# A two-layer cross-attention and mixture-of-experts kernel: work moved between engines in the first routing, unread products, row stores and key transfers placed anew

## The reference, cut to what matters

```python
x = x + xattn(layernorm(x), ctx, ctx, ...)      # layer 0 attention, 16 heads of 8, 32 x 64 rows of 128
x = x + ffn0(layernorm(x), w_gate, w_g, w_u, w_d)  # routing: top 2 of 8 experts, softmax of the two
x = x + xattn(layernorm(x), ctx, ctx, ...)      # layer 1 attention
x = x + ffn1(layernorm(x), gate_w, W1, b1, W2, b2) # routing again, hidden 512, exact gelu, biases

def ffn1(x):
    topk_vals, topk_idx = top_k(xf @ gate_w, 2);  topk_w = softmax(topk_vals)
    comb = zeros.at[rows, topk_idx].add(topk_w)
    h = gelu(einsum('nd,edf->enf', xf, W1) + b1[:, None, :])
    return einsum('ne,end->nd', comb, einsum('enf,efd->end', h, W2) + b2[:, None, :])
```

## Time and profile before

| | us |
|---|---|
| median of 3 runs | 430.56 |
| runs | 435.54, 429.47, 430.56 |
| the profiled execution | 428.84 |
| its span, first to last instruction | 427.0 |
| PE busy in the span | 365.1 (85%) |
| DVE busy | 341.2 (80%) |
| ACT busy | 268.8 (63%) |
| POOL busy | 245.7 (58%) |

### The profile page before, as it was taken

The page is one execution under the profiler, slowest core; times in us unless marked ns, Lnnn a source line. Parts: engine busy times, 40 slices in busy tenths (PEclk is TensorE's granted clock), DMA queues, the critical chain, the costliest instruction groups (busy, mean ns, idle before and its releaser), DMA issues.

```text
span 427.0 us, 12926 instructions
## 1 busy us (share of the span) xinstructions
PE 365.1 (85%) x4528; PEld 256.8 (60%) x4528; DVE 341.2 (80%) x978; ACT 268.8 (63%) x591; POOL 245.7 (58%) x362
## 2 busy tenths in 40 slices
PE   3977799998779999999998799898878899999900
PEld 2644566666446656666655567676634798888800
DVE  6876589998888787887876689988877899999707
ACT  3664588987457555666556788786722766767504
POOL 7860367777525558576661244456787356677630
PEclk9996899999999999999999999998996999999965
DMA  7358797000001111101002400001113223232136
GB/s 202 83 166 257 218 382 266 4 3 2 2 0 51 51 52 49 48 16 40 0 11 34 62 3 2 5 21 34 40 47 102 78 79 95 78 90 65 45 103 223
DMA packets 30837, 33.15 MB, mean 78 GB/s; under 512 B 3908, under 2 KB 22606, under 8 KB 30776
## 3 DMA queue, kind: packets, MB, share of 16 engines
q1 hardware_dynamic: 27164, 25.84, 21.2%
q0 software_dynamic: 2496, 5.18, 3.6%
q10 hardware_dynamic: 1116, 1.31, 1.0%
HBM read 15.22 MB, written 15.01 MB: 71 GB/s over the span
## 4 chain that ended last, share of the span: by engine, by line
PE 48%; DVE 17%; SPq 10%; issue 10%; POOL 9%; ACT 3%; DMA 2%; POOLq 0%; DVEq 0%; ACTq 0%
PE ps L1433 10%; PE ps L1435 9%; PE ps L1434 9%; SPq L353 5%; PE ps L1681 4%; PE ps L1529 3%; DVE area L1026 3%; POOL sorted_rows L783 3%; POOL area L819 2%; PE ps L1602 2%; PE ps L1815 1%; SPq L371 1%; POOL expert_sums L839 1%; PE ps L1835 1%; PE ps L1443 1%
## 5 line engine op out<-in xcount | busy, mean ns | idle before, releaser
L819 POOL TENSOR_TENSOR area<-area 128x512 f16<-128x512 f32 x44 | 51.0, 1159 | 41.8 <-ACT area L587 41.8
L839 POOL DMA_INDIRECT expert_sums<-area x46 | 49.7, 1081 | 27.1 <-ACT area L609 14.4
L1433 PE MATMUL ps<-w,area 128*128 128x128 f16 (+1 forms) x360 | 63.7, 219 | 0.3 <-POOL area L819 0.2
L1434 PE MATMUL ps<-w,area 128*128 128x128 f16 (+1 forms) x360 | 63.7, 219 | 0.0
L1435 PE MATMUL ps<-w,area 128*128 128x128 f16 (+1 forms) x360 | 63.7, 219 | 0.0
L1433 PE MATMUL ps<-area,w 128*128 128x512 f16 (+1 forms) x180 | 58.8, 327 | 3.1 <-DVE area L1349 1.4
L1434 PE MATMUL ps<-area,w 128*128 128x512 f16 (+1 forms) x180 | 58.5, 325 | 0.0
L1435 PE MATMUL ps<-area,w 128*128 128x512 f16 (+1 forms) x180 | 58.4, 325 | 0.0
L1026 DVE TENSOR_REDUCE area<-ps 128x8 f32<-128x512 f32 x64 | 41.2, 686 | 14.5 <-PE ps L1681 13.2
L583 ACT ACTIVATE area<-ps 128x512 f32<-128x512 f32 x44 | 26.1, 597 | 35.1 <-PE ps L1435 34.5
L633 ACT ACTIVATE area<-ps,b_now 128x256 f32<-128x256 f32 x92 | 36.2, 477 | 12.0 <-PE ps L1435 11.9
(11 more groups left out here) (241 smaller groups left out, 1039.4 us busy)
## 6 DMA issues: line engine op xcount, KB each, us to landing
sorted_rows<-filler_rows SPq DMA_DIRECT2D x16, 528.0 KB, 6.3
w_stage<-in_L_ffn_W SPq DMA_DIRECT2D x8, 512.0 KB, 4.0
w<-sorted_rows SPq DMA_DIRECT2D x23, 132.0 KB
keys<-area SPq DMA_DIRECT2D x32, 48.0 KB
area<-in_ctx SPq DMA_DIRECT2D x4, 256.0 KB, 4.8
keys<-expert_sums SPq DMA_DIRECT2D x4, 256.0 KB, 5.4
keys<-expert_sums ACTq DMA_DIRECT2D x4, 256.0 KB, 6.2
out<-x_res SPq DMA_DIRECT2D x8, 128.0 KB, 1.9
```

What stands on the lines that cost most here:

```text
L819: nc.gpsimd.tensor_tensor(hid[:, n % 4, 1, :], gated[:, n % 4, :], hid[:, n % 4, 0, :], ALU.subtract).then_inc(q["lo"], 1)
L839: nc.gpsimd.indirect_dma_start(out=expert_sums, out_offset=bass.IndirectOffsetOnAxis(ap=to_row[:, j, h:h + 1], axis=0), in_=ys[j % OUTS][: ...
L1433: pe.matmul(dst, lhs[0], rhs[0], start=start, stop=False, **kw)
L1434: pe.matmul(dst, lhs[0], rhs[1], start=False, stop=False, **kw)
```

## The change

It has seven parts.

1. SP: `place_keys(0, 1)` is issued before the five tables and the first two weight chunks of layer 1, not behind them.
2. PE: 21 unread products are added between the projections and step 0 of attention 0 (2+2 in `project_queries`, 4 at the start, 6+2 in step -2, 2 in step -1, 3 in step 0). Fewer in the end of attention 1 (9 to 4, but 5 to 8 later) and at the start of `experts1` (7 to 3, 4 to 3).
3. ACT and POOL: `output_bias_rows` goes from the routing into steps 8 to 14 of the dense feed-forward, in three pieces (ACT) and four (POOL).
4. The lower halves of parts 0, 1 and 2 are made by PE (`take_part`: minus the upper half added to the bank) and ACT (`routing_low`), and no longer by DVE.
5. DVE: `rank` of part 0 stays in step 15, of part 1 goes behind the statistics of step 16, of part 2 behind the statistics of tile 15.
6. POOL: each entry of `STORED` comes one step earlier, and step 16 ends at 21 scatters, not 20.
7. DVE: `statistics(15)` before `row_shift(14)`; the late table in two, its second part behind `arrive(0)` and `arrive(1)`; `shares` behind the loop of `experts1`.

```diff
-STORED = {8: 2, 9: 4, 10: 6, 11: 9, 12: 11, 13: 14, 14: 16, 15: 18, 16: 20}
+STORED = {7: 2, 8: 4, 9: 6, 10: 8, 11: 11, 12: 13, 13: 16, 14: 18, 15: 20, 16: 21}
...
+            place_keys(0, 1)
             for dst, name in ((iota8, "iota8"), (expert_rows, "expert_rows"), (table, "table"), (before16, "before16"), (filler_rows, "filler")):
...
             load_chunk(1)
 
-            place_keys(0, 1)
...
+                    if l == 0 and t == TILES - 1:
+                        routing_low(F[l], 2)
...
                         routing_high(F[l], 2)
+                        routing_low(F[l], 0)
+                        routing_low(F[l], 1)
...
+            def routing_low(q, p):
+
+                t0, t1 = PARTS[p]
+                act.wait_ge(q["xt_sub"], p + 1)
+                nc.scalar.activation(xTa[:, 1, t0 * P:t1 * P], ps[:, part_bank[p], 0:(t1 - t0) * P], ACT.Copy).then_inc(q["xt_lo"], 1)
...
             def routing(l):
                 q = F[l]
-                output_bias_rows()
...
+                    if 8 <= n <= 10:
+                        output_bias_rows(n - 8)
...
-            def output_bias_rows():
-
-                pool.wait_ge(s["rs"], 2 * TILES)
+            def output_bias_rows(k):
+
+                e = slice(2 * k, 2 * k + 2)
                 pool.wait_ge(s["b2"], 34)
-                nc.gpsimd.tensor_tensor(b2_rows[32:33, :, :], b2_raw[32:33, :, :], b2_hi[32:33, :, :], ALU.subtract).then_inc(s["b2"], 1)
-                pool.wait_ge(s["b2"], 35)
+                pool.wait_ge(F[0]["lo"], 12 + k)
+                nc.gpsimd.tensor_tensor(b2_rows[32:33, e, :], b2_raw[32:33, e, :], b2_hi[32:33, e, :], ALU.subtract).then_inc(s["b2"], 1)
+                pool.wait_ge(s["b2"], 35 + k)
...
+                if 11 <= n <= 14:
+                    output_bias_rows(n - 11)
...
                     row_shift(LAST)
                     early_tiles()
-                    statistics(LAST + 1)
...
-                late_table()
-                shares()
+                tiles_left()
                 arrive(0)
                 arrive(1)
+                late_table()
...
+                if l == 0 and g >= 2:
+                    unread_products(2, 0, 0, 512)
                 pe.wait_ge(KV["xt"], n + 1)
...
+                        pe.wait_ge(KV["v_lo"], 2 * GROUPS)
+                        unread_products(6, 5, 0, 512)
+                    if l == 0 and t == 0:
+                        unread_products(3, 6, 0, 512)
...
                         turn_part(l, 2)
+                        take_part(l, 0)
+                        take_part(l, 1)
...
+            def take_part(l, p):
+
+                q = F[l]
+                t0, t1 = PARTS[p]
+                pe.wait_ge(q["xt_hi"], p + 1)
+                pe.matmul(ps[:, part_bank[p], 0:(t1 - t0) * P], minus_ident16, xTa[:, 0, t0 * P:t1 * P], start=False, stop=True,
+                          skip_group_check=True).then_inc(q["xt_sub"], 1)
...
-                unread_products(7, 5, 0, 512)
+                unread_products(3, 5, 0, 512)
                 turn(0)
                 turn(1)
-                unread_products(4, 6, 0, 512)
+                unread_products(3, 6, 0, 512)
```

More of the change, by code:

```diff
@@ L260, in build @@
         F = [sems("xh xt_ps xt_hi lg_ps lg top idx ex pr up act hi lo down "
-                  + ("gu xd xt_lo oh cb c16 ct_ps ct_a ct_d res t1 gt", "sa a16 rk_ps rk bs place tbl b1_ps b1 slots_ps xs_hi xs_lo gate y "
+                  + ("gu xd xt_sub xt_lo oh cb c16 ct_ps ct_a ct_d res t1 gt", "sa a16 rk_ps rk bs place tbl b1_ps b1 slots_ps xs_hi xs_lo gate y "
                      "tok nm wq sc ld0 ld1 ld2 ld3 so0 so1 so2 so3 so4 so5 so6 so7 sum0 sum1 sum2 sum3 add")[l], f"_f{l}") for l in range(2)]
@@ L557, in sort_rows @@
                 nc.scalar.activation(act_warm[:, 1:2], minus_half[:, :], ACT.Gelu)
[L559 to L565 removed]
+            def output_bias_rows(k):
+                if k == 0:
+                    act.wait_ge(s["b2"], 32)
+                    nc.scalar.activation(b2_rows[0:1, :, :], b2_raw[0:1, :, :], ACT.Copy, scale=WSCALE)
+                elif k == 1:
+                    nc.scalar.activation(b2_hi[32:33, :, :], b2_raw[32:33, :, :], ACT.Copy, scale=WSCALE).then_inc(s["b2"], 1)
+                else:
+                    act.wait_ge(s["b2"], 33)
+                    nc.scalar.activation(b2_raw[32:33, :, :], b2_raw[32:33, :, :], ACT.Copy, scale=WSCALE).then_inc(s["b2"], 1)
             def routing(l):
                 q = F[l]
[L569 removed]
                 routing_high(q, 3)
@@ L1004, in step @@
                         outputs(t - 1)
-                    if l == 0 and t == TILES - 1:
-                        low(F[l], 2)
-                    if l == 0 and t == TILES:
-                        rank(F[l], 1)
                     if alive(t + 1):
@@ L1012, in step @@
                         statistics(t - 2)
-                    if l == 0 and t == TILES - 2:
-                        low(F[l], 0)
-                    if l == 0 and t == TILES - 2:
-                        low(F[l], 1)
                     if l == 0 and t == TILES - 1:
@@ L1019, in step @@
                     if l == 0 and t == TILES:
-                        rank(F[l], 2)
+                        rank(F[l], 1)
                     if alive(t + 3):
@@ L1052, in last_steps @@
                     residual(LAST + 1)
+                    statistics(LAST + 1)
                     row_shift(LAST)
                     early_tiles()
-                    statistics(LAST + 1)
                     row_shift(LAST + 1)
@@ L1064, in attention @@
                     statistics(TILES - 1)
+                    rank(F[l], 2)
                 else:
@@ L1371, in experts1 @@
                         arrive(j + 2)
+                shares()
                 dve.wait_ge(q["pr"], 4)
@@ L1616, in step @@
                         scores(t + 3, (t + 3) % 2, 1).then_inc(q["s_ps"], 1)
+                    if l == 0 and t == -2:
+                        unread_products(2, 5, 0, 512)
+                    if l == 0 and t == -1:
+                        pe.wait_ge(s["bo"], 2)
+                        unread_products(2, 6, 0, 512)
                     if alive(t + 1) and turned_by_pe(l, t + 1):
@@ L1634, in step @@
                         weigh_values(t)
+                    if l == 0 and t == TILES - 2:
+                        take_part(l, 2)
                 def last_steps():
```

21 lines of the change are left out of this document (9 added, 12 removed).

## The result

| | before | changed |
|---|---|---|
| runs | 435.54, 429.47, 430.56, 429.43, 427.44 | 424.18, 421.83, 422.21, 422.44, 422.04 |
| median | 429.47 | 422.21 |
| the profiled execution | 428.84 | 424.18 |

The ratio is 0.984 (95% interval 0.981 to 0.988), a gain of 1.6%; the prediction was 422.0 us. Four more runs on another chip (run `again`) gave 0.979 (0.974 to 0.984), median 421.27. So the changed kernel is faster by 1.6 to 2.1%, on either side of what was called two per cent.

A forecast was written before the change was run, and what follows sets the result against it. PE 85% and DVE 80% busy, so only seams between stages can win. 3.9 + 2.0 + 2.4 = 8.3 off 428.84 gives 420.5; 1.7 more for a median gives 422.2, rounded to 422; own range 419.5 to 424.

The forecast's parts named there:

- Parts 1 and 2, 3.9: Start of attention 0: earlier keys and added unread products save 3.9 us, bounds 0.7 and 4.5.
- The whole 2.37 us goes: Start of attention 0: with keys there by 45.6, PE's 2.37 us standstill before tile 4's scores disappears.
- 0.86: Start of attention 0: without a standstill the clock drop after it goes, maxima spacing 4.92 to 4.06, saving 0.86 us.
- 0.75: Start of attention 0: with the unread products, tile 3's maxima come 0.75 us sooner.
- Parts 3 to 5, 2.0: First routing: tile 15 turned at 114.2 instead of 116.23, saving 2.0 us, bounds 1.5 and 2.7.
- I give them 0, and 0.2 us against them: First routing: moving the lower halves off DVE gains 0 and costs 0.2 us, as `take_part` 2 precedes PE's 6 products.
- Parts 2, 6 and 7, 2.4: Start of `experts1`: `up(2)` comes 2.4 us sooner, set by DVE's late table, bounds 1.0 and 3.3.
- the 24th scatter ends 2.5 sooner: POOL before `experts1`: the 24th scatter ends at 320.6, 2.5 us sooner, so the first load issues at 322.1.
- The clock falls at `up(2)`: Second rival, `experts1`: PE idles some 2 us, one tile at half clock costs 2.6; 424.4 us, chance 0.10.
- The prologue stays at half clock: Rival, start of attention 0: products at half clock, gain 0.7 for 3.9; 425.4 us, chance 0.11.
- The keys do not come sooner: Last rival, start of attention 0: key DMAs stall until weights land, part 1 gives 1.0; 425.2 us, chance 0.04.
- Slow for long: Rival, `experts1`: clock stays low beyond `up(2)`; with seven slow tiles 440 us, chance 0.04.

The follow-up runs named there:

- `again`: The changed kernel with no edit, run once more for a second profile: ratio to the kernel before 0.979, median 421.27 us.
- `experts`: Kernel before with only parts 6 and 7 and the fewer unread products at the end: ratio 0.995, 2.0 us.
- `bias_only`: Kernel before with only the ACT and POOL bias pieces moved to the feed-forward: median 429.41 us, ratio interval 0.995 to 1.003.
- `bias_back`: Changed kernel with the output bias rows put back in the routing, POOL's as one piece: median 421.07 us, ratio to the kernel before 0.977.
- `keys`: Kernel before with only the last 16 key DMAs moved ahead of the tables: ratio 1.001 (0.997 to 1.005).
- `few_split`: Changed kernel with 3 instead of 11 unread products before tile 15's turn and `tile_experts` moved ahead of `arrive(0)`: median 421.78 us, ratio to the kernel before 0.980.
- `old_fill`: Changed kernel with 7 and 4 unread products at the start of `experts1` instead of 3 and 3: 422.05, 422.16, 428.40, 428.45 us, no ratio.

## Why the prediction was right, point by point

**The time.** 422.0 was said, 422.21 came, in the range and in its own range. The sum, 8.3, was made for one execution against another, and so compared (second profile) it is 8.2: 4.4, 2.5, 2.0 for 3.9, 2.0, 2.4. The total is better than its terms, and that it is met to some tenths is luck: by the medians the gain is 7.3 us in the first comparison (429.47 to 422.21, where the forecast had started from 430.56) and 9.4 in the second (430.65 to 421.27), and one term was met only because of the execution that the rows came from, as follows.

**Parts 1 and 2, 3.9.** The marks came as said: keys by 41.3 (43.3 at most was the bound), scores of tile 4 at 46.54 (46.1), 4.06 between maxima, clock 1.00 throughout. What was wrong is to whom the gain belongs. "The whole 2.37 us goes" and 0.86 with it were booked to the keys, 0.75 to the products; alone the keys give 0 and the products 0 by the time of the kernel, and their A of 22.02 and 22.23 lies inside that of the old start, 21.43 to 23.01. The step that failed is to price the removal of a wait at its length while the stretch ahead of it ran at half clock. Also the 23.01 us of the kernel before is its slowest A of four with the same code there (21.43, 21.47, 21.49): against the other three the seam is worth 2.9, not 3.9 or 4.4. In those three PE has no wait for keys at all, since it works at half clock until they are there. So the 2.37 us that the prediction removes stood in one of four profiles, and that 3.9 lies between 2.9 and 4.4 is luck of the profile. The same code has its low clock in another place each time; windows of `experts`, and of the kernel before:

```profile
39.00:48.00 9.00, 8.95 (x93) 5.60 (x94) 5.84 (x15) 5.63 (x12) 2.19 (x6) 0.50 0.52 96
```
```profile
42.00:48.00 6.00, 4.22 (x65) 2.66 (x64) 4.22 (x10) 4.55 (x10) 3.06 (x6) 1.00 0.48 78
```

The prediction also reads the earlier trace rows as a low clock behind sparse windows and full clock where PE is busy without a break. The rows themselves have PE busy for 3.25 of 3.30 us and 4.00 of 4.00 at 0.50, and for 0.51 of 1.03 at 1.00. The sparse stretch is the one ahead of the low clock, in the kernel before:

```profile
30.00:33.00 3.00, 1.59 (x33) 0.91 (x30) 1.91 (x6) 1.55 (x5) 0.33 (x1) 1.00 1.15 341
33.00:34.70 1.70, 0.15 (x3) 0.00 (x0) 1.05 (x2) 0.00 (x0) 0.42 (x2) 0.74 1.10 297
```

The Trainium skill (TensorE: Matmul & The Clock Gate, Part 1: The HAM clock gate) has the clock halved after too little activity. The trace agrees in kind: 0.50 behind PE's waits with the keys or the products alone, 1.00 with both.

**Parts 3 to 5, 2.0.** It was 2.4 to 2.5. The fill of 11 products bound next, as said, and cutting it gave another 0.66. The mis-sized term is "I give them 0, and 0.2 us against them" for the lower halves: they were worth 0.36 in favour, presumably since DVE gets to the statistics of tiles 14 and 15 that much sooner. The 2.4 to 2.5 stood in the bounds of 1.5 to 2.7. That normalising runs without POOL beside it follows from the moved pieces and from the new order, each by itself (`bias_only`, `bias_back`); the prediction saw only the first.

That the 2.24 us of normalising are POOL's doing is shown: 2.24 or 2.25 in five kernels where POOL's piece ran beside it, 0.34 or 0.35 in the nine others, with the same wait in front in `bias_only`. The Trainium skill (SBUF — State Buffer, Who interferes with whom) has this port pair as an exclusive lock, and the trace agrees that one of the two is held up. Which of them had the ports first the rows don't settle: DVE's starts 0.05 us ahead of POOL's (113.84, 113.89), and yet it is DVE's that is long. By that rule the pieces in the feed-forward could hold up each weight split by 0.53 us; one of the two splits beside them took 0.81 us as before and the other 1.07 instead of 0.93, and nothing behind them moved.

**The bias pieces.** Cost 0 in the feed-forward was right for PE and the residuals. Their size was not: 0.93, 0.93, 0.66 and 0.66 us on POOL for 0.53. A quarter of the row takes more than a quarter of the time (0.66 for 2.12 / 4), and the two of 0.93 stand beside a weight split of DVE (142.81 to 143.62, 144.87 to 145.94), the two of 0.66 don't:

```profile
143.22 0.93 POOL L805 TENSOR_TENSOR b_rows<-q_T 1x256 f16<-1x256 f32 x1
...
147.84 0.66 POOL L805 TENSOR_TENSOR b_rows<-q_T 1x256 f16<-1x256 f32 x1
```

**Parts 2, 6 and 7, 2.4.** The chain came as worked out: the first load 5.82 us behind the factors for 7.12, the late table open on DVE for 2.24 us, then PE waiting for `arrive(2)`. The size holds as a sum of like stretches (1.1 up to the factors, where 1.25 was said, and 1.4 behind them), and the D of `experts` is 2.39 below before. Two things were missed. The step "the 24th scatter ends 2.5 sooner" was followed only to the first load; the last eight scatters come no sooner, and they are the next bound. And some 0.8 of the win is a clock that returns earlier, which one of five profiles of the old code (`keys`) also has; so without it about 1.7 is left (1.1 + 1.4 - 0.8). Whether the change itself brings the earlier return is open: in the other four profiles of the old code the clock is back 13.2 to 14.9 us behind the factors, in `keys` 10.6, and in the new code no low stretch of this place lasts beyond 12.6. By medians of D (111.6 old, 110.9 new, without `few_split`), in which the drops of attention 1 are mixed, 0.7 is left of 2.4.

**The rivals.** "The clock falls at `up(2)`" came true in the first profile (0.74 in 328 to 332, 91.37 for 90.69 in the table above, 0.7 us) and not in the second (1.00). It did so in one of the eight profiles of the new code, and not in `old_fill`, where PE's wait is as long (2.50 us for 2.55) behind a thicker fill. It is cheaper than the 2.4 of the rival; that PE would soon have met the late rows of the sixth tile anyway fits this, but was not tried. "The prologue stays at half clock" did not happen with both parts, but it is just what the keys alone do. "The keys do not come sooner" did not happen: the first of them took 1.16 us to issue, and all were issued by 41.30. Slow for long: in none of the new kernels.

**Slips in the sums.** They change nothing above 0.2 us. In part 2, 3.1 and 0.86 are 4.0, but 0.9 less 0.25 is also 0.65 and not 0.75, and the two cancel. In parts 3 to 5 a fill of 11 products at 0.23 is 2.5 and not 2.4, so the sum should have said 1.9. At `experts1`, `up(0)` began at 330.35 and not 330.56. In the second rival 422.2 and 2.4 are 424.6, in the last one 422.2 and 2.9 are 425.1.

## What to carry to other kernels

A wait of TensorE ahead of which the clock is low was not worth its length here. Read the granted clock on both sides; if two holes lie close together, close both before judging either: alone, each gave nothing. Measure a seam by the distance between two marks in the trace (0.03 us here) rather than by the time of the kernel (some 2 us), but only where the clock is at its full level in both traces, and with more than one profile of the kernel before: its slowest A was 1.5 us above the other three. When two engines collide, ask which of two reorderings already parts them before paying for both.

## What the runs showed that was not expected

The projections and the attention of layer 1 up to the maxima of tile 15 (stretch C) took 78.0 to 80.8 us in twelve profiles, and 83.6 in that of `bias_only`, 4.0 us above the median of its kernel; where it is long, there are stretches at half clock which come at different places. The two profiles of the changed kernel had PE busy for 4.01 and 4.24 of the 6 us from 228 to 234 us at full clock, and just behind it the first fell to half (0.50 from 236 to 244) while the second did not. What decides it is open. This lottery, 2.8 us in one stretch without `bias_only`, is more than what the first routing or the start of `experts1` gave.

The long issue on SP is not the small table's own: moved behind the keys, the table fell from 4.40 to 0.44 us. The time went to what is issued at that point instead: 2.77 us on the third weight load in the first profile, and 3.33 us on the first of the keys in `again`, where the other keys take 0.69.
